# Products of x with the output's weights: from the recurrence's steps to the outputs, on one core

## What is computed

```
def step(c, xt):
    ft = sigmoid(xt @ wf.T + c @ uf.T + bf)
    it = sigmoid(xt @ wi.T + c @ ui.T + bi)
    gt = tanh(xt @ wc.T + c @ uc.T + bc)
    return ft * c + it * gt
c_final = scan(step, c0, x)
h = tanh(einsum('tbi,oi->tbo', x, wo) + c_final @ uo.T + bo)
x = layernorm(x + h)
```

## Time and profile before

| | |
|---|---|
| median of three executions | 2189.14 us |
| traced execution, its own time | 2190.01 us |
| its span in the trace | 2188.2 us |
| PE busy | 2107.5 us, 96% |
| DVE busy | 1633.3 us, 75% |
| ACT busy | 1470.2 us, 67% |
| PE's share of the chain that ended last | 89% |
| steps and outputs | from 1798.24 us to the end |

### The profile page before, as it was taken

The page is one execution under the profiler, slowest core; times in us unless marked ns, Lnnn a source line. Parts: engine busy times, 40 slices in busy tenths (PEclk is TensorE's granted clock), DMA queues, the critical chain, the costliest instruction groups (busy, mean ns, idle before and its releaser), DMA issues.

```text
span 2188.2 us, 41691 instructions
## 1 busy us (share of the span) xinstructions
PE 2107.5 (96%) x16608; PEld 1139.3 (52%) x16608; DVE 1633.3 (75%) x2099; ACT 1470.2 (67%) x1766; POOL 134.4 (6%) x186
## 2 busy tenths in 40 slices
PE   6999999999999999999999999999999879999995
PEld 3444444444444444444444444444444348888873
DVE  6788888888888888888888888888888833333347
ACT  2777777777777777777777777787777653333338
POOL 0000000000000000000000000000000000000005
PEclk8999999999999999999999999999999989999998
DMA  4222222222222222222222222222222302000007
GB/s 109 55 57 55 67 55 66 55 64 55 65 56 66 56 65 56 64 56 64 56 63 64 55 64 55 64 55 64 55 55 54 91 28 69 29 20 28 29 10 259
DMA packets 91252, 134.14 MB, mean 61 GB/s; under 512 B 21301, under 2 KB 43573, under 8 KB 91077
## 3 DMA queue, kind: packets, MB, share of 16 engines
q1 hardware_dynamic: 66948, 97.91, 17.6%
q10 hardware_dynamic: 24128, 33.79, 4.8%
HBM read 37.77 MB, written 16.78 MB: 25 GB/s over the span
## 4 chain that ended last, share of the span: by engine, by line
PE 89%; ACT 4%; DVE 3%; issue 2%; DMA 1%; SPq 1%; ACTq 0%; POOL 0%; DVEq 0%; POOLq 0%
PE pv_ps L722 21%; PE pair_ps L658 17%; PE work L626 15%; PE banks L1176 12%; PE pair_ps L684 12%; PE work L788 3%; PE pair_ps L634 3%; ACT probs L391 2%; PE banks L1199 2%; DVE maxes L581 1%; PE banks L1233 1%; PE banks L1169 1%; PE work L792 1%; DVE res L563 1%; ACT summed L1044 1%
## 5 line engine op out<-in xcount | busy, mean ns | idle before, releaser
L581 DVE TENSOR_REDUCE maxes<-pair_ps 128x2 f32<-128x1024 f32 x1024 | 1228.0, 1221 | 240.5 <-PE pair_ps L634 153.9
L391 ACT ACTIVATE probs<-pair_ps,small 128x1024 f32<-128x1024 f32 x512 | 563.1, 1113 | 227.1 <-PE pair_ps L634 225.6
L391 ACT ACTIVATE probs<-pair_ps 128x1024 f32<-128x1024 f32 x512 | 516.8, 1024 | 160.0 <-PE pair_ps L658 154.8
L722 PE MATMUL pv_ps<-probs,vals 128*32 128x512 f32 x4096 | 547.3, 606 | 0.6 <-ACT probs L391 0.6
L658 PE MATMUL pair_ps<-q_op,k_op 56*128 56x512 f32 (+1 forms) x2048 | 479.6, 477 | 15.4 <-ACT probs L391 11.5
L684 PE MATMUL pair_ps<-k_op,q_op 55*128 55x512 f32 x2048 | 434.1, 432 | 6.7 <-ACT probs L391 4.5
L658 PEld LDWEIGHTS pair_ps<-q_op,k_op 56*128 56x128 f32 (+1 forms) x2048 | 191.7, 184 | 446.9 <-DVE maxes L581 204.7
L684 PEld LDWEIGHTS pair_ps<-k_op,q_op 55*128 55x128 f32 x2048 | 196.0, 186 | 151.4 <-issue 107.3
L634 PE MATMUL pair_ps<-eye_b,tri_b 64*128 64x64 bf16 x4096 | 163.0, 194 | 0.0
L634 PEld LDWEIGHTS pair_ps<-eye_b,tri_b 64*128 64x128 bf16 x4096 | 93.8, 96 | 114.6 <-issue 93.3
L722 PEld LDWEIGHTS pv_ps<-probs,vals 128*32 128x32 f32 x4096 | 80.7, 108 | 98.3 <-issue 87.3
(11 more groups left out here) (161 smaller groups left out, 2450.5 us busy)
## 6 DMA issues: line engine op xcount, KB each, us to landing
k_op<-kq_h SPq DMA_DIRECT2D x508, 64.0 KB, 2.2
q_op<-kq_h SPq DMA_DIRECT2D x256, 64.0 KB, 2.2
k_op<-kq_l SPq DMA_DIRECT2D x254, 64.0 KB, 2.2
x_step<-in_xT ACTq DMA_DIRECT2D x16, 512.0 KB, 3.9
q_op<-kq_l SPq DMA_DIRECT2D x128, 64.0 KB, 2.2
x_res<-in_x ACTq DMA_DIRECT2D x16, 512.0 KB, 4.0
x_dram<-res ACTq DMA_DIRECT2D x16, 512.0 KB, 2.9
x_back<-x_dram SPq DMA_DIRECT2D x16, 512.0 KB, 5.4
```

Source lines behind the costliest of these rows:

```text
L391: act.activation(probs[:, s % 2, 2 * hp:2 * hp + 2, :], pairs_ps[pair_of(b, s, "b", hp)][:, :, :], ACT.Exp, scale=LAM if s // 4 % 2 else 1 ...
L581: dve.reduce_max(maxes[:, u % 2, :, hp, s % 4], pairs_ps[pair_of(b, s, "a", hp)][:, :, :], mybir.AxisListType.X).then_inc(a_reduced, 1)
L722: last = pe.matmul(pv_ps[32 * h:32 * h + 32, :], vals[:, c, g // 2, att, at:at + 32], probs[:, s % 2, h, :], start=(c == 0), stop=(c == TC ...
```

## The change

`hidden` and `keep_hpre` are gone, and with them `hpre`. The high and low parts of all 16 x stay in SBUF (`xs`, 128 KB of every partition), and `output_from_x(t)` does the 24 matmuls with `wo` straight into the output's pair of banks, where `keep_in_banks(t)` had stood. To make room, `x_back`, `summed` and `co_h` now lie where the gates' weights and `act_out` lie in the steps, and a tanh is written over the high parts of its own x (`tangents`). So the first four loads to `x_back` now wait for the last gate product of the last step (`gate_full`, 6T), and the first high part of x waits until all eight pieces of weights are split (`w_lo`). A turn waits for the low part of the x before it (`xs_lo`) instead of `hp_done`. All `Fori` loops on PE, ACT, DVE and POOL are written out.

```
-            sp.wait_ge(shared.x1_stored, 16 + 16 * B)
+            sp.wait_ge(shared.x1_stored, 16 + 16 * B)
+            sp.wait_ge(gate_full, 6 * T)
             for t in range(BACK):
                 sp.dma_start(x_back[:, t, :, :], shared.tokens(x1[t])).then_inc(in_back[t], 16)
...
+            if (t, k) == (0, 0):
+                act.wait_ge(w_lo, len(pieces))
+            act.activation(xt_h[t][:, k, :], step_bank(t, k), ACT.Copy).then_inc(xs_hi, 1)
...
             for k in range(KC):
-                if not first:
-                    pe.wait_ge(hp_done, t * 2)
+                if t > 1:
+                    pe.wait_ge(xs_lo, t * 2 - 1 + k)
...
-            for i in range(2):
-                hidden(i)
-            gates_from_x(pe, 0, (4, 5), True)
-            turn_step(pe, 1, False)
-            with pe.Fori(0, T - 2) as t:
-                from_state(t)
-                from_x(t + 1)
-                turn_step(pe, t + 2, False)
-            from_state(T - 2)
-            from_x(T - 1)
-            from_state(T - 1)
+            gates_from_x(pe, 0, (4, 5))
+            turn_step(pe, 1)
+            for t in range(T):
+                from_state(t)
+                if t + 1 < T:
+                    gates_from_x(pe, t + 1, range(GATES * KC))
+                if t + 2 < T:
+                    turn_step(pe, t + 2)
...
-            def keep_in_banks(t):
-                for i in range(2):
-                    pe.matmul(out_ps[t % BACK][:, i, :], id_sb[:, :], hpre[:, t, 2 * i:2 * i + 2, :].rearrange("p c n -> p (c n)"),
-                              start=True, stop=False)
+            def output_from_x(t):
+                for c in range(TC):
+                    for k in range(KC):
+                        for a, d in parts:
+                            pe.matmul(out_ps[t % BACK][:, c // 2, H * (c % 2):H * (c % 2) + H], (xt_h, xt_l)[a][t][:, k, P * c:P * c + P],
+                                      (wo_h, wo_l)[d][:, 0, k, :], start=(c % 2 + k + a + d == 0), stop=False)
```

More of the change, by code:

```diff
@@ L925, in __init__ @@
         pieces += [(uc_h[:, g, :, :], uc_l[:, g, :, :], 0.5) for g in range(GATES)] + [(wo_h[:, 1, :, :], wo_l[:, 1, :, :], 0.5)]
[L927 to L934, removed]
+        step_bank = lambda t, k: gate_ps[4 + k] if t == 0 else work[k]
         def sync(sp):
             sp.wait_ge(shared.x1_stored, 16 + 16 * B)
+            sp.wait_ge(gate_full, 6 * T)
             for t in range(BACK):
@@ L1009, in scalar @@
             act.wait_ge(shared.x1_stored, 16 + 16 * B)
-            def step(t, more, further, load):
+            for t in range(T):
                 for n in range(5):
@@ L1016, in step @@
                 state_hi(t, 1)
-                if more:
-                    keep_hpre(t + 1)
-                if further:
+                if t + 2 < T:
                     step_hi(act, t + 2, 0)
                     step_hi(act, t + 2, 1)
-                if load:
+                if t + 3 < T:
                     load_step(act, t + 3)
[L1025 to L1029, removed]
             for c in range(TC):
@@ L1045, in normalise @@
                                    scale=rstd[:, i, c:c + 1]).then_inc(normed, 1)
[L1047 to L1055, removed]
         def weight_lo(dve, n):
@@ L1104, in state_lo @@
                 dve.tensor_tensor(s_l[:, k, :], state[:, k, :], s_h[:, k, :].bitcast(F32), ALU.subtract).then_inc(s_lo, 1)
-            keep_hpre(0)
             step_lo(dve, 1, 0)
             step_lo(dve, 1, 1)
-            def step(t, more, further):
+            for t in range(T):
                 keep_state(t, 0)
@@ L1130, in vector, with add_x @@
                 dve.tensor_tensor(co_l[:, c, :], share[c], co_h[:, c, :].bitcast(F32), ALU.subtract).then_inc(co_lo, 1)
-            def add_x(r, i, first):
-                t = r * BACK + i
+            def add_x(t):
+                i = t % BACK
                 dve.wait_ge(tanh_done, t + 1)
[L1135 to L1155, removed]
@@ L1178, in gates_of, with gates_from_x @@
             return last
-        def gates_from_x(pe, t, gates, first):
-            if first:
+        def gates_from_x(pe, t, gates):
+            if t == 0:
                 pe.wait_ge(w_lo, len(pieces))
-                pe.wait_ge(xs_lo, 2)
+            pe.wait_ge(xs_lo, t * 2 + 2)
             for n in gates:
-                if not first:
+                if t:
                     pe.wait_ge(gate_done, t * 6 - 5 + n)
                 for k in range(KC):
-                    gates_of(pe, n, k, (wx_h, wx_l), (xt_h, xt_l), k == 0, False)
+                    gates_of(pe, n, k, (wx_h, wx_l), (xt_h[t], xt_l[t]), k == 0, False)
         def tensor(pe):
[L1193 to L1204, removed]
-                for i in range(2):
-                    hidden(i)
-                gates_from_x(pe, t, range(GATES * KC), False)
             def from_state(t):
@@ L1256, in tensor @@
                 if c == 0:
[L1257 removed]
+                    pe.wait_ge(xs_lo, 2 * T)
                 if c == 2:
```

99 lines of the change are left out of this document (56 added, 43 removed).

## The result

| | before | after |
|---|---|---|
| median | 2188.94 us (2187.09 to 2189.32, four runs) | 2157.46 us (2155.48 to 2157.82, four runs) |
| traced execution, its own time | 2190.01 us | 2155.48 us |
| its span | 2188.2 us | 2153.6 us |

The ratio of the times is 0.9856, with an interval of 0.9839 to 0.9873: 31.5 us less at the medians, where 37.3 were forecast. The forecast of 2151.9 us was 5.6 us too low, and the time lies inside the range.

A forecast was written before the change was run, and what follows sets the result against it. PE was taken to bound the steps, and the circle through the stores the outputs. Steps gave 46.2 us, outputs gave back 8.9: net -37.3 from 2189.14, so 2151.9 us, range 2147.5 to 2159.5.

The forecast's parts named there:

- What bounds the kernel: Whole kernel: PE holds 89% of the chain and sets the steps' pace; something slower than PE sets the outputs'.
- the circle: Outputs before: sum, scales, normalising, store and the sum three outputs on take 10.23 us, 3.41 for one output.
- Steps: Recurrence and lead-in: `hidden` leaves 15 turns (43.05 us) and the lead-in (3.14 us), 46.19 us, with nothing else late.
- Loops: Loops written out: a possible gain from 13 backward branches on PE, counted as zero.
- Outputs: Outputs: 24 matmuls of 2.87 us replace `keep_in_banks`; PE needs 3.80 us per output, 65.78 in all, and sets the pace.
- The term of 8.9: Outputs to the end of the span: 65.78 + 13.1 = 78.9 us instead of 69.96, giving back 8.9.
- One sign that was named for a wrong forecast: Outputs: groups of 24 matmuls taking over 3 us would show the forecast wrong.
- First loads: Start of the outputs: the four loads to `x_back`, now issued later, stay hidden with 2.9 us to spare.
- The circle of stores: Rival, outputs: stores over 4.98 us still set the pace; with 8.1 us stores +14.6, 2166.5 us; chance 0.09.
- late once: Rival: a one-time delay from late first loads or late-fetched program costs 8.1 us, giving 2160.0; chance 0.06.
- the steps keep their length: Rival, steps: `hidden` was cover, turns stay 20.35 us and 43.05 us come back, 2195.0; chance 0.02.
- the clock fell: Rival, outputs: waits for `tanh_done` let PE's clock fall, doubling 53.2 us, 2205.1; chance 0.01.

The follow-up runs named there:

- e5: Changed kernel with only the high by high products in the outputs, 8 of 24 matmuls: 2145.43 us, ratio 0.9799.
- e7: Changed kernel with the 24 products with `wo` also done, unused, in each of 15 steps: 2199.82 us, ratio 1.0047.
- e1: Changed kernel with `xs` alone moved by 928 bytes of padding: 2151.55 us, ratio 0.9831.
- e2: Changed kernel with 928 bytes of padding under the parts of both the state and x: 2147.68 us, ratio 0.9818.
- e10: Changed kernel with the gates' weights moved by 1120 bytes and the parts of the state and x by 2048: 2146.96 us, ratio 0.981.
- e4: Kernel before with every loop of the recurrence and outputs written out, nothing else: 2188.89 us, ratio 1.0007.
- e9: Changed kernel with the first four loads to `x_back` held back until the state's share is split: 2155.47 us, ratio 0.9847.
- e11: Changed kernel with 480 bytes of padding under the parts of the state and x: 2154.28 us, ratio 0.9843.
- e3: Changed kernel with 32 bytes of padding under the parts of the state and x: 2154.19 us, ratio 0.9835.
- e12: e8's kernel with the products for output 0 moved ahead of the eight bias matmuls: 2147.56 us, ratio 0.9816.
- e6: Changed kernel with `LEAD = 2` instead of 3, normalising one tanh earlier in ACT's program: 2154.88 us, ratio 0.984.
- e8: Changed kernel with 928 bytes of padding under the parts of the state and x, and `LEAD = 2`: 2146.34 us, ratio 0.9806.

## Why the prediction was right, and where it was off

*What bounds the kernel* held: the steps on PE, the outputs on something slower than PE in the kernel before and on PE in the changed one. e5 brings the pace of before back by taking PE's work away. e7 gives the products back to the steps, and the gain is gone. One reading of the circle was off without touching its sum: the scales that let ACT normalise at 2162.39 are not those of the sum at 2158.07 but of the output before it, since DVE's program has the sum of output t + 1 ahead of the last statistics of output t. That is why the circle spans three outputs and not the four of the buffers.

*Steps.* `hidden` left the path without a wait in its place; no wait of PE stands in the chain of the steps. The term was right in its mechanism and 3.7 us too large in size: 39.3 and not 43.05, because the gate products of x take 16.86 - 8.42 = 8.44 us at their new place in SBUF and not 8.19 (15 x 0.25 = 3.75). I had taken their duration as that of a shape. e1 brings back this part, e2 and e10 more than it. The lead-in gave 3.10 of the forecast's 3.14.

*Loops.* Counting zero was right (e4, ratio 1.0007). The rule of the Trainium skill (Runtime: NRT & Kernel Launch, Instruction fetch mechanics), that a taken branch can stall an engine, makes no visible difference here: the turn of 20.35 us is the same with a backward branch and without one (e4).

*Outputs.* PE's part was forecast as 65.78 us and took 67.2; without the 1.5 us at half clock it is 65.7. The 24 products took 2.88 and not 2.87, and each output 3.80. The tail was 12.7 us, with 13.1 forecast. The term of 8.9 came out as 9.97: the half clock behind the bias matmuls, which I had not looked for, added 1.5, and the shorter tail took 0.4 back. The last sum came 2.0 us after the last product and not 2.5. One sign that was named for a wrong forecast did appear, once: the first group of 24 took 3.72 us, over 3.

*First loads.* Right that they are hidden, wrong in the room: 2.9 us were worked out from the slowest landing and for the last of the four loads, while the first sum needs only the first. In e9 that load was issued at 2083.36 and the sum ran from 2087.29, and the room is over 9 us.

*The rivals.* The circle of stores needed stores over 4.98 us; the slowest took 3.8, in less traffic, as argued. Nothing was late once, nor did the steps keep their length. Apart from the stretch behind the bias, the clock fell ahead of the last product in the outputs of e5 only, where PE waits; in the changed kernel PE doesn't, and the clock is 1.00 but for the 3.4 us. That rival's condition, PE waiting for `tanh_done`, was therefore not met. The stretch behind the bias is another case, since PE did not wait there.

*The sum.* The span fell by 34.6 us, 2.7 less than forecast: 3.7 in the steps and 1.1 in the outputs are missing, and 2.2 came in ahead of the lead-in. The rest, down to the 31.5 of the medians, comes from which executions were traced: that of before lies 1.07 us over its median, that of after 1.98 below its own.

That the time lies inside the range is in part luck. The measured 2157.46 is at the upper end of the forecast's own bounds (2151.9 + 4.3 + 1.4 = 2157.6), but those belong to the 24 products and the tail, which came out as forecast. What moved the time, the gate products' pace and the half clock, had no bound in the sum.

The fastest version that computes the whole result is the changed kernel with the moving operands placed by e2 or e10, with or without `LEAD = 2`: 0.9806 to 0.9818 of the time before, whose intervals overlap, and 0.4 to 0.5% less than the changed kernel. The steps then take 265.7 to 266.0 instead of 273.65 us.

## What to carry to other kernels

When work goes from the engine that bounds a stage to another stage, ask which engine sets the pace of each, in periods: here 2.87 us went from each of 15 steps at full price, and 2.87 - 1.72 = 1.15 us more for each output cost only the 0.5 (3.80 - 3.33) by which PE passed the pace that the outputs had before, and a longer way to the first output. A duration of a matmul read from a trace belongs to its operands' places as well as to its shape, so a change that lays out memory anew may move it by 3%, and such a layout can be tried with a pad of some hundred bytes. A wait that is visible but off the path, as those for the stores (12.7 us in all), gave 0.2 to 0.5 us when it was taken away.

## What the runs showed of the hardware, unexpected

**The pace of 512-column fp32r matmuls depends on where the moving operand lies relative to the weights.** Worked out from the starts of the products of x in the steps, one matmul each:

| distance of moving operand to weights, modulo 2048 bytes | kernels | ns per matmul |
|---|---|---|
| 0 | before (x), e1 (x), e2, e10 | 226.7 |
| 448 | e11 | 233.3 |
| 896 | e3 | 232.4 |
| 928 | after | 234.3 |

The products of the state in the kernel before, also at 928, took 8.42 us for 36 where those of x took 8.19. The offsets were counted from the order and sizes of the allocations, up to the start of each tensor. The weights of one matmul begin 0, 512, 1024 or 1536 bytes behind that start. In the state's products, the matmuls of the last three kinds took 226.7 ns each in e2, and 234.4, 234.4 and 235.0 in the changed kernel (those of the first kind have the start of a group among them). So all four kinds go together, and the distances may as well be read modulo 512 bytes: 0, 448, 384 and 416 in the order of the table. Groups of 256 columns don't follow it: 24 take 2.88 after, 2.86 in e2 and e10, 2.84 in e3, 2.83 in e11. Why the distance matters, whether the period is shorter still, and what other distances give, stays open.

**A stretch at 1.2 GHz behind eight one-row matmuls, with PE busy.** It begins 0.4 to 1.3 us behind the bias matmuls (0.7 in the changed kernel) and ends after 3.4 us. What PE did before it was those eight matmuls, 1.92 us, at full clock, and they stand in all 14 traces. It is there in the traces of after, e3, e4, e5, e7 and e12, and not in those of before, e1, e2, e6, e8, e9, e10 and e11: 6 of 14. In e8, which doesn't have it, the same place (share of the state and output 0) ran at full clock in heavier traffic:

```profile
2068.00:2071.40 3.40, 3.40 (x31) 3.40 (x30) 1.02 (x2) 0.63 (x1) 0.00 (x0) 1.00 0.99 387
```

So traffic alone (348 GB/s in the stretch of after) doesn't bring it. Nor is traffic needed: in e4 the stretch has none.

```profile
2119.00:2122.40 3.40, 3.40 (x10) 1.85 (x9) 0.69 (x1) 0.63 (x1) 0.00 (x0) 0.50 0.00 0
```

The Trainium skill (TensorE: Matmul & The Clock Gate, Part 1: The HAM clock gate) says that activity releases the throttle; by its records PE was active here, and still slow for 3.4 us. What decides between the six and the eight is open.

**What comes ahead of the lead-in differs from execution to execution.** The lead-in's part that changes began at 1798.24 in the trace of before and at 1796.08 after, but at 1796.06 in e4, whose program up to there is that of before, and at 1801.39 in e1, whose program is that of after with a pad. So the 2.16 us that came in ahead of the lead-in belong to an execution and not to the change. The granted clock is below 1.00 in all these traces between 1780 and 1800 us (0.74 before, 0.76 after), and such stretches may be what moves the program; that is not shown. The runs of one kernel lie 2.3 us apart for the changed kernel and up to 7.7 in e4.
